# Softmax sums of the first attention with tokens on partitions, 16 reciprocals for each token, widened by GpSimd and turned by TensorE

## The chip, the core and the metric

One core of one Trainium2 chip runs the whole program in one launch. The metric is the device time of one execution in microseconds (us), the median of several runs. The engines are named as the profile names them: PE (TensorE), PEld (its weight loads), DVE (VectorE), ACT (ScalarE), POOL (GpSimd) and SP (SyncE). Each works through its own instructions in the order in which they are written and waits at semaphores for the others.

## The reference

The program is four layers of attention and feed-forward on x of 16 x 64 tokens with 128 features. Only the first attention is touched. Of it this is computed, with 16 heads of 8 features and 64 keys for each batch:

```
qh = (layernorm(x) @ Wq.T + bq)   kh = (ctx @ Wk.T + bk)   vh = (ctx @ Wv.T + bv)
scores = einsum('bhqd,bhkd->bhqk', qh, kh) / sqrt(8)
attn = softmax(scores, axis=-1)
out = einsum('bhqk,bhkd->bhqd', attn, vh)      (heads side by side: 128 features)
x = x + out @ Wo.T + bo
```

The rest of the model follows: a mixture of experts, a channel attention, a quantized matmul, a deformable attention, experts again, a masked attention and a quantized gated network. All in float32.

## The kernel before

The 1024 tokens are 8 tiles of 128. A tile is called here by its number j, and its work is spread over five consecutive rounds t of a software pipeline, `attention()` from L409, which each engine goes through in its own loop:

- Scores of tile t+1: PE multiplies queries and keys (L487), 8 matmuls, in round t.
- In round t DVE takes each head's maximum (L610) and subtracts it (L613). ACT takes the exponential of the whole tile (L552).
- In round j+1 PE turns the probabilities, so that keys lie on partitions (L501, 8 transposes), and ACT copies them from PSUM in two halves (L563) into one of two buffers `pT`.
- In round j+2 PE weighs the values (L514, 16 small matmuls, result `ps[:, 6, 0:128]`, features on partitions, tokens along the row) and makes the softmax sums (L518, 8 matmuls with a 32-column stationary operand of ones and `pT` as the moving operand of 128 columns). The sums come out in the layout of the result: each head's sum is repeated on the head's 8 partitions, for 128 tokens.
- In round j+3 DVE takes the reciprocal of 128 x 128 sums (L635) and multiplies it into the result (L637, `o_fm`). PE multiplies with Wo (L543, into `ps[:, 7]`).
- In round j+4 DVE adds the result to x (L643), and in j+5 it takes the statistics for the next layer norm (L252).

The order is the order of the code. Within a round DVE goes: scores of t, reciprocal and product of t-3, addition of t-4, statistics of t-5. PE goes: scores of t+1, transposes of t-1, values and sums of t-2, and last the projection of t-3. PE begins the values of tile j only when DVE has read tile j-1 out of that PSUM bank (semaphore `of_ready`). The hooks `experts_pe`, `experts_act` and `experts_dve` put the start of the following layer into the last rounds: the layer norm of the first 512 tokens (its second square root and DVE's factors in rounds 7 and 8, ACT's two tiles L349 in round 8), its turn on PE (L367) at the end of round 8, and the first experts' matmuls (L852, L857) at the end of round 9. The projection of tile 7 is behind those on PE. The expert layer after it is emitted in one piece and starts with a second block of L852/L857.

The branch `masked` of this function is not used in this program: the last attention has code of its own.

Of the kernel before, what the change touches and what calls it, by code (L numbers as in the profile page):

```python
# [20 lines left out]
P = 128  # L21
B, S, D = 16, 64, 128
T = B * S
NT = T // P
H, HD = 16, 8
# [90 lines left out]
def build(nc, A, out):  # L116

    ctx = ExitStack()
    with ctx:
# [130 lines left out]
        def tile_stats(j):  # L250

            return V.bn_stats(stats[:, j, :], x_tm[:, j, :])  # L252
# [156 lines left out]
        def attention(n, layer, wq, wo, bo, prepared, masked, bm_ready=None, beside_pe=nothing, beside_act=nothing,  # L409
# [18 lines left out]
            of_ready, y_ready, y_added = s("o_fm"), s("y"), s("y_added")  # L428

# [25 lines left out]
            else:  # L455
                @block.gpsimd
                def _(pool):

                    l0_norm.wait(pool)
                    pool.wait_ge(rows0_in, 16)  # L460
                    pool.wait_ge(v_sb, 4)
                    G.tensor_tensor(x_tm[:], x_tm[:], over(row(bo), 1, NT), ALU.add).then_inc(pool_chain, 1)
                    chained["pool"] += 1

# [3 lines left out]
            def _(pe):  # L468
# [36 lines left out]
                def weigh_values(j):  # L505
                    pe.wait_ge(pt_ready, 2 * j + 2)
                    if j == 0:
                        pe.wait_ge(vx_ready, 4)
                    else:
                        pe.wait_ge(of_ready, j)  # L510
# [6 lines left out]
                    for c in range(8):  # L517
                        ins = PE.matmul(ps[32 * (c // 2):32 * (c // 2) + 32, 6, 128:256], ones[:, c % 2, :],  # L518
                                        pT[j % 2][:, 128 * c:128 * c + 128], start=(c % 2 == 0), stop=(c % 2 == 1))
                    ins.then_inc(o_ready, 1)  # L520

# [4 lines left out]
                for t in range(NT + 3):  # L526
# [11 lines left out]
                    if 0 <= t - 3 < NT:  # L538
                        j = t - 3
                        pe.wait_ge(of_ready, j + 1)  # L540
                        if j >= 1:
                            pe.wait_ge(y_added, j)
                        PE.matmul(ps[:, 7, 0:128], o_fm[:, j * P:j * P + P], mat(wo), start=True, stop=True)\  # L543
                            .then_inc(y_ready, 1)
# [3 lines left out]
            def _(act):  # L548
                for t in range(NT + 2):
# [7 lines left out]
                    if 0 <= t - 1 < NT:  # L557
# [3 lines left out]
                        for k in range(2):  # L561
                            act.wait_ge(ptT_ready, 2 * j + k + 1)
                            AC.activation(pT[j % 2][:, 512 * k:512 * k + 512], ps[:, 4 + k, :], ACT.Copy)\  # L563
                                .then_inc(pt_ready, 1)
                    beside_act(act, t)
# [15 lines left out]
            def _(dve):  # L581
# [3 lines left out]
                for t in range(NT + 5):  # L585
                    if t < NT:
# [40 lines left out]
                    if 0 <= t - 3 < NT:  # L627
                        j = t - 3
                        dve.wait_ge(o_ready, j + 1)
                        if masked:  # L630

                            dve_link(V.tensor_scalar(rb, ps[:, 6, 128:256], 1.0, None, ALU.max))
                            V.reciprocal(rb, rb).then_inc(rb_ready, 1)
                        else:
                            V.reciprocal(rb, ps[:, 6, 128:256]).then_inc(rb_ready, 1)  # L635
                        dve.wait_ge(rb_ready, j + 1)
                        V.tensor_tensor(o_fm[:, j * P:j * P + P], ps[:, 6, 0:128], rb, ALU.mult).then_inc(of_ready, 1)  # L637
                    if 0 <= t - 4 < NT:
                        j = t - 4
                        if j == 0 and not masked:  # L640
                            dve.wait_ge(pool_chain, 2)
                        dve.wait_ge(y_ready, j + 1)
                        V.tensor_tensor(x_tm[:, j], x_tm[:, j], ps[:, 7, 0:128], ALU.add).then_inc(y_added, 1)  # L643
                    if 0 <= t - 5 < NT and t - 5 != 3:
                        dve.wait_ge(y_added, t - 4)
                        ins = tile_stats(t - 5)
                    if t - 4 == 3:
                        dve.wait_ge(y_added, 4)
                        dve_link(tile_stats(3))
# [2243 lines left out]
```

## Time and profile before

| | us |
|---|---|
| median of 3 runs (lowest, highest) | 464.21 (463.15, 467.38) |
| the profiled execution's own time | 463.37 |
| its span in the profile | 461.6 |
| PE busy | 398.0 (86%) |
| DVE busy | 359.8 (78%) |
| ACT busy | 253.0 (55%) |
| POOL busy | 114.5 (25%) |

The span is the profiled execution from its first to its last instruction; 1.8 us lie around it. The first attention's rounds take the stretch from about 14 to 56 us. Busy shares are those of the whole program; what the change is worth is read from that stretch alone. Matmuls overlap, so how long a group of them takes is read from the start of its first to the start of the group behind it, when nothing waits in between.

### The profile page before, as it was taken

How to read it: one execution, taken by the hardware profiler on the slowest of the kernel's cores; microseconds unless marked ns; L12 is line 12 of the kernel's file. 1: busy time of each engine (PE TensorE's matmuls, PEld its weight loads, DVE VectorE, ACT ScalarE, POOL GpSimd, SP SyncE). 2: the span in 40 equal slices, each digit the busy share in tenths (PEclk: the TensorE clock that was granted, in tenths of full speed). 3: DMA queues.
4: the chain of work that ended last, by engine and by line, in shares of the span. 5: the costliest groups of instructions: out<-in, count | busy, mean ns of one | idle time of the engine just before them, and what ended most of it. 6: DMA issues, size and time to landing. Idle time of an engine off the chain costs nothing.

```text
span 461.6 us, 8687 instructions
## 1 busy us (share of the span) xinstructions
PE 398.0 (86%) x3415; PEld 262.4 (57%) x3415; DVE 359.8 (78%) x802; ACT 253.0 (55%) x438; POOL 114.5 (25%) x97
## 2 busy tenths in 40 slices
PE   8988989999999988786787888899999999868156
PEld 5555566566666667553454546385556766643045
DVE  4799646558544587979879898999899689988985
ACT  4785753333223334456797784766766433444942
POOL 3200000006990001005995544031221023100200
PEclk9999999999999999989999999999999999989759
DMA  7890000000000000017000003000000000000001
GB/s 227 357 322 6 1 1 1 1 0 1 0 1 0 1 3 2 0 58 309 2 1 0 3 1 70 0 2 0 2 0 3 1 1 3 1 0 0 1 1 45
DMA packets 11084, 16.51 MB, mean 36 GB/s; under 512 B 5274, under 2 KB 9764, under 8 KB 10148
## 3 DMA queue, kind: packets, MB, share of 16 engines
q1 hardware_dynamic: 10756, 15.17, 9.4%
q10 hardware_dynamic: 288, 0.79, 0.6%
q8 instruction: 27, 0.44, 0.4%
q14 instruction: 13, 0.11, 0.1%
HBM read 15.43 MB, written 0.52 MB: 35 GB/s over the span
## 4 chain that ended last, share of the span: by engine, by line
PE 48%; DVE 32%; ACT 11%; issue 7%; DMA 1%; POOL 0%; ACTq 0%; DVEq 0%
PE ps L852 7%; PE ps L857 7%; PE ps L891 7%; PE ps L2119 4%; PE ps L2109 2%; PE ps L242 2%; DVE arena L1906 2%; DVE stats L252 2%; PE ps L1758 2%; PE ps L2146 1%; DVE arena L610 1%; DVE arena L613 1%; PE ps L2662 1%; DMA ctx_fm<-in_ctx_fm 1%; PE ps L2643 1%
## 5 line engine op out<-in xcount | busy, mean ns | idle before, releaser
L970 DVE SCALAR_TENSOR_TENSOR arena<-ps,cols,arena 128x512 f32<-128x512 f32 x40 | 29.7, 750 | 42.3 <-PE ps L857 38.0
L866 ACT ACTIVATE arena<-ps,cols 128x512 f32<-128x512 f32 x40 | 27.4, 687 | 63.9 <-PE ps L852 63.8
L242 PE MATMUL ps<-const 128*128 128x256 f32 x162 | 43.0, 412 | 7.4 <-ACT arena L2709 4.4
L891 PEld LDWEIGHTS ps<-weights,arena 128*128 128x128 f32 x320 | 38.6, 192 | 8.1 <-issue 8.0
L1906 DVE TENSOR_SCALAR arena<-ps 128x512 f32<-128x512 f32 x56 | 36.4, 683 | 7.3 <-PE ps L1744 3.5
L242 PEld LDWEIGHTS ps<-const 128*128 128x128 f32 x162 | 31.4, 203 | 16.3 <-ACT arena L2709 4.7
L891 PE MATMUL ps<-weights,arena 128*128 128x128 f32 x320 | 39.2, 276 | 0.2 <-DVE x_tm L959 0.2
L857 PE MATMUL ps<-h_fm,weights 128*128 128x512 f32 x80 | 37.7, 593 | 0.7 <-DVE arena L970 0.7
L852 PE MATMUL ps<-h_fm,weights 128*128 128x512 f32 x80 | 37.7, 594 | 0.6 <-ACT h_fm L373 0.6
L2109 PE MATMUL ps<-h_fm,weights 128*128 128x512 f32 x64 | 30.3, 606 | 2.7 <-ACT arena L2493 1.8
L1744 PE MATMUL ps<-l2buf,picks_b 128*128 128x256 bf16 x160 | 25.5, 275 | 6.5 <-DVE arena L1906 4.7
L2119 PEld LDWEIGHTS ps<-weights,arena 128*128 128x128 f32 x256 | 29.4, 192 | 2.6 <-issue 2.6
L2119 PE MATMUL ps<-weights,arena 128*128 128x128 f32 x256 | 30.0, 275 | 0.9 <-DVE x_tm L2336 0.9
L857 PEld LDWEIGHTS ps<-h_fm,weights 128*128 128x128 f32 x80 | 15.1, 190 | 20.2 <-issue 18.2
L1758 PE MATMUL ps<-arena,kexp 128*32 128x320 f32 x256 | 20.5, 438 | 5.3 <-ACT l2buf L1849 3.9
L1065 POOL TENSOR_TENSOR wn<-wn,winv 128x1152 f32<-128x1152 f32 x1 | 2.1, 2129 | 85.7 <-DVE winv L1055 85.7
L2493 ACT ACTIVATE arena<-ps 128x512 f32<-128x512 f32 x32 | 18.0, 597 | 9.2 <-PE ps L2109 9.1
L959 DVE SCALAR_TENSOR_TENSOR x_tm<-ps,arena,x_tm 128x128 f32<-128x128 f32 x80 | 22.4, 342 | 0.3 <-DVE stats L252 0.2
L1744 PEld LDWEIGHTS ps<-l2buf,picks_b 128*128 128x128 bf16 x160 | 12.6, 99 | 17.0 <-DVE arena L1906 10.0
L2109 PEld LDWEIGHTS ps<-h_fm,weights 128*128 128x128 f32 x64 | 11.2, 189 | 17.7 <-issue 10.2
L852 PEld LDWEIGHTS ps<-h_fm,weights 128*128 128x128 f32 x80 | 13.7, 191 | 10.4 <-issue 9.6
L2275 POOL TENSOR_TENSOR arena<-arena 128x1024 f32<-128x1024 f32 x5 | 11.5, 2301 | 31.6 <-DVE arena L2374 31.6
(401 smaller groups left out, 890.8 us busy)
## 6 DMA issues: line engine op xcount, KB each, us to landing
weights<-in_moe_w SPq DMA_DIRECT2D x2, 2048.0 KB, 10.0
weights<-in_moe_w SPq DMA_DIRECT2D x3, 1280.0 KB
l2buf<-in_picks SPq DMA_DIRECT2D x1, 1664.0 KB, 7.9
rows<-in_rows SPq DMA_DIRECT2D x1, 1024.0 KB, 13.7
x_tm<-in_x SPq DMA_DIRECT2D x2, 256.0 KB, 5.2
ctx_fm<-in_ctx_fm ACTq DMA_DIRECT2D x1, 512.0 KB, 5.9
ctx_tm<-in_ctx SPq DMA_DIRECT2D x1, 512.0 KB, 14.5
mats<-in_mats SPq DMA_DIRECT2D x1, 512.0 KB, 14.8
```

The lines of the kernel that those rows point to most:

```text
L242: PE.matmul(ps[:, bank, 0:256], ident, const[:, 0:256], start=True, stop=True)
L852: PE.matmul(ps[:, k, :], w1[:, e, P * k:P * k + P], h_fm[:, t], start=True, stop=True)\
L857: PE.matmul(ps[:, 2 + k, :], w2[:, e, P * k:P * k + P], h_fm[:, t], start=True, stop=True)\
L866: AC.activation(silu[:, k, :], ps[:, k, :], ACT.Silu, bias=bias_col(0, e, k)).then_inc(silu_ok, 1)
L891: ins = PE.matmul(ps[:, 4 + u % 2, P * t:P * t + P], glu[:, u % 2, k, P * t:P * t + P], w3[:, e, k, :], start=(k == 0), stop=(k == 1))
L959: ins = V.scalar_tensor_tensor(out=x_tm[:, j], in0=ps[:, 4 + u % 2, P * t:P * t + P], scalar=gates[:, j, e:e + 1], in1=x_tm[:, j], op0=ALU ...
L970: V.scalar_tensor_tensor(out=glu[:, u % 2, k, :], in0=ps[:, 2 + k, :], scalar=bias_col(1, e, k), in1=silu[:, k, :], op0=ALU.add, op1=ALU.m ...
L1744: ins = PE.matmul(ps[:, m % 3, 256 * i:256 * i + 256], picks_b[:, 2 * c + i, :], ixm[:, hg, 256 * half:256 * half + 256], start=True, stop ...
L1758: ins = PE.matmul(ps[32 * hl:32 * hl + 32, 4 + par, 0:NK * S], kvc[:, j, 4 * hg + hl, :], hats[:, u % 2, NK * hl:NK * hl + NK, S * (2 * i ...
L1906: V.tensor_scalar(hat_rows(u, c), ps[:, m % 3, :], 0.0, 1.0, ALU.max, ALU.min).then_inc(near_ok, 1)
L2109: PE.matmul(ps[:, n % 3, :], m2w1[:, e, P * k:P * k + P], h_fm[:, 0:T2], start=True, stop=True)\
L2119: ins = PE.matmul(at_ps, hid[:, e % 2, k, P * j:P * j + P], m2w2[:, e, k, :], start=(k == 0), stop=(k == 3))
```

## The change

- The sums change sides. 8 matmuls now have a 128 x 128 piece of `pT` as the stationary operand and two columns of ones as the moving one (`head_ones`, two heads in each piece). They write 16 columns, `ps[:, 6, 128:144]`: one sum for each token and head, with tokens on partitions.
- ACT copies the unnormalized result to `o_fm` and the 16 sums to `shares[j % 2]` as soon as PE has made them, in round j+2, behind its copies of `pT`. A new semaphore `kept` tells PE that the bank is free, and DVE that the sums are there.
- DVE takes the reciprocal of 128 x 16 at the head of round j+3.
- POOL widens the 16 reciprocals to 128 columns (`rb`), 8 instructions in all.
- PE turns `rb` with a matmul against the identity (`spread_shares`) into `ps[:, 7, 0:128]`, between the sums of tile j+1 and the projection of tile j. The projection's result goes to the same place of PSUM.
- DVE multiplies it into `o_fm` as its last step on scores in round j+3.
- DVE's addition to x and its statistics move ahead of its work on the scores of the same round.

```diff
--- before.py
+++ after.py
@@ -426,6 +426,10 @@
             ptT_ready, pt_ready = s("probsT"), s("probsT_sb")
             o_ready, rb_ready = s("o_ps"), s("sums")
             of_ready, y_ready, y_added = s("o_fm"), s("y"), s("y_added")
+            kept, rep_ps = s("kept"), s("shares_ps")
+            shares = [arena[:, 6176 + H * i:6176 + H * i + H] for i in range(2)]
+            head_ones = ones[:, 0, 0:2 * HD:HD]
+            widened = []
 
 
             if masked:
@@ -461,6 +465,14 @@
                     pool.wait_ge(v_sb, 4)
                     G.tensor_tensor(x_tm[:], x_tm[:], over(row(bo), 1, NT), ALU.add).then_inc(pool_chain, 1)
                     chained["pool"] += 1
+                    for j in range(NT):
+                        pool.wait_ge(rb_ready, j + 1)
+                        if j >= 1:
+                            pool.wait_ge(rep_ps, j)
+                        G.tensor_copy(rb.rearrange("p (h d) -> p h d", h=H), over(shares[j % 2], 2, HD))\
+                            .then_inc(pool_chain, 1)
+                        chained["pool"] += 1
+                        widened.append(chained["pool"])
 
 
 
@@ -507,7 +519,7 @@
                     if j == 0:
                         pe.wait_ge(vx_ready, 4)
                     else:
-                        pe.wait_ge(of_ready, j)
+                        pe.wait_ge(kept, j)
                     for b in range(2):
                         for c in range(8):
                             g = c // 2
@@ -515,9 +527,15 @@
                                       pT[j % 2][:, 128 * c + 64 * b:128 * c + 64 * b + 64],
                                       start=(c % 2 == 0), stop=(c % 2 == 1))
                     for c in range(8):
-                        ins = PE.matmul(ps[32 * (c // 2):32 * (c // 2) + 32, 6, 128:256], ones[:, c % 2, :],
-                                        pT[j % 2][:, 128 * c:128 * c + 128], start=(c % 2 == 0), stop=(c % 2 == 1))
+                        ins = PE.matmul(ps[:, 6, 128 + 2 * c:130 + 2 * c], pT[j % 2][:, 128 * c:128 * c + 128], head_ones,
+                                        start=True, stop=True)
                     ins.then_inc(o_ready, 1)
+
+                def spread_shares(j):
+                    pe.wait_ge(pool_chain, widened[j])
+                    if j >= 1:
+                        pe.wait_ge(y_added, j)
+                    PE.matmul(ps[:, 7, 0:128], rb, ident, start=True, stop=True).then_inc(rep_ps, 1)
 
                 scores(0)
                 l0_norm.wait_turned(pe)
@@ -537,9 +555,8 @@
                         transposes(t - 1)
                     if 0 <= t - 3 < NT:
                         j = t - 3
+                        spread_shares(j)
                         pe.wait_ge(of_ready, j + 1)
-                        if j >= 1:
-                            pe.wait_ge(y_added, j)
                         PE.matmul(ps[:, 7, 0:128], o_fm[:, j * P:j * P + P], mat(wo), start=True, stop=True)\
                             .then_inc(y_ready, 1)
                     beside_pe(pe, t)
@@ -562,6 +579,13 @@
                             act.wait_ge(ptT_ready, 2 * j + k + 1)
                             AC.activation(pT[j % 2][:, 512 * k:512 * k + 512], ps[:, 4 + k, :], ACT.Copy)\
                                 .then_inc(pt_ready, 1)
+                    if 0 <= t - 2 < NT:
+                        j = t - 2
+                        act.wait_ge(o_ready, j + 1)
+                        AC.activation(o_fm[:, j * P:j * P + P], ps[:, 6, 0:128], ACT.Copy)
+                        if j >= 2:
+                            act.wait_ge(pool_chain, widened[j - 2])
+                        AC.activation(shares[j % 2], ps[:, 6, 128:128 + H], ACT.Copy).then_inc(kept, 1)
                     beside_act(act, t)
 
             if masked:
@@ -583,6 +607,22 @@
                     guard_queries(dve, 0)
                     dve.wait_ge(bm_ready, NT)
                 for t in range(NT + 5):
+                    if 0 <= t - 3 < NT:
+                        j = t - 3
+                        dve.wait_ge(kept, j + 1)
+                        V.reciprocal(shares[j % 2], shares[j % 2]).then_inc(rb_ready, 1)
+                    if 0 <= t - 4 < NT:
+                        j = t - 4
+                        if j == 0 and not masked:
+                            dve.wait_ge(pool_chain, 2)
+                        dve.wait_ge(y_ready, j + 1)
+                        V.tensor_tensor(x_tm[:, j], x_tm[:, j], ps[:, 7, 0:128], ALU.add).then_inc(y_added, 1)
+                    if 0 <= t - 5 < NT and t - 5 != 3:
+                        dve.wait_ge(y_added, t - 4)
+                        ins = tile_stats(t - 5)
+                    if t - 4 == 3:
+                        dve.wait_ge(y_added, 4)
+                        dve_link(tile_stats(3))
                     if t < NT:
                         pr = prob[t % 3].rearrange("p (g h k) -> p g h k", g=4, h=4)
                         pr3 = prob[t % 3].rearrange("p (h k) -> p h k", h=H)
@@ -626,27 +666,9 @@
                         V.tensor_scalar(prob[j % 3], prob[j % 3], 0.0, None, ALU.max).then_inc(clean, 1)
                     if 0 <= t - 3 < NT:
                         j = t - 3
-                        dve.wait_ge(o_ready, j + 1)
-                        if masked:
-
-                            dve_link(V.tensor_scalar(rb, ps[:, 6, 128:256], 1.0, None, ALU.max))
-                            V.reciprocal(rb, rb).then_inc(rb_ready, 1)
-                        else:
-                            V.reciprocal(rb, ps[:, 6, 128:256]).then_inc(rb_ready, 1)
-                        dve.wait_ge(rb_ready, j + 1)
-                        V.tensor_tensor(o_fm[:, j * P:j * P + P], ps[:, 6, 0:128], rb, ALU.mult).then_inc(of_ready, 1)
-                    if 0 <= t - 4 < NT:
-                        j = t - 4
-                        if j == 0 and not masked:
-                            dve.wait_ge(pool_chain, 2)
-                        dve.wait_ge(y_ready, j + 1)
-                        V.tensor_tensor(x_tm[:, j], x_tm[:, j], ps[:, 7, 0:128], ALU.add).then_inc(y_added, 1)
-                    if 0 <= t - 5 < NT and t - 5 != 3:
-                        dve.wait_ge(y_added, t - 4)
-                        ins = tile_stats(t - 5)
-                    if t - 4 == 3:
-                        dve.wait_ge(y_added, 4)
-                        dve_link(tile_stats(3))
+                        o = o_fm[:, j * P:j * P + P]
+                        dve.wait_ge(rep_ps, j + 1)
+                        V.tensor_tensor(o, ps[:, 7, 0:128], o, ALU.mult).then_inc(of_ready, 1)
                     if t - 5 == 7:
                         dve_link(ins)
                     beside_dve(dve, t)
```

What stands on DVE in round 5, before and after the change (line numbers of each kernel; L610/L650 and L613/L653 are maxima and subtraction). Before:

```order
L610 TENSOR_REDUCE arena<-ps 128x2x4 x2
L613 TENSOR_TENSOR arena<-ps,arena 128x2x256 x2
L635 RECIPROCAL arena<-ps 128x128
L637 TENSOR_TENSOR o_fm<-ps,arena 128x128
L643 TENSOR_TENSOR x_tm<-x_tm,ps 128x128
L252 BN_STATS stats<-x_tm 128x6
```

After:

```order
L613 RECIPROCAL arena<-arena 128x16
L619 TENSOR_TENSOR x_tm<-x_tm,ps 128x128
L252 BN_STATS stats<-x_tm 128x6
L650 TENSOR_REDUCE arena<-ps 128x2x4 x2
L653 TENSOR_TENSOR arena<-ps,arena 128x2x256 x2
L671 TENSOR_TENSOR o_fm<-ps,o_fm 128x128
```

The reciprocal, the addition and the statistics stand now ahead of the maxima, and the product alone is left behind the subtraction.

PE in one round with scores, before, from the scores to the projection:

```order
L487 MATMUL ps<-kexp,q_fm 64x256 x8
L501 MATMUL ps<-const,arena 128x128 x8
L514 MATMUL ps<-arena,v 32x64 x16
L518 MATMUL ps<-arena,const 32x128 x8
L543 MATMUL ps<-mats,o_fm 128x128
```

After:

```order
L499 MATMUL ps<-kexp,q_fm 64x256 x8
L513 MATMUL ps<-const,arena 128x128 x8
L526 MATMUL ps<-arena,v 32x64 x16
L530 MATMUL ps<-const,arena 128x2 x8
L538 MATMUL ps<-const,arena 128x128
L560 MATMUL ps<-mats,o_fm 128x128
```

L530 (the sums) has 2 moving columns on 128 x 128 instead of 128 moving columns on 32 stationary ones, and L538 is new, between the sums and the projection L560.

ACT from round 4 on; before it has the exponential (L552) and the two copies of `pT` (L563) in each round:

```order
L552 ACTIVATE arena<-arena 128x1024
L563 ACTIVATE arena<-ps 128x512 x2
L552 ACTIVATE arena<-arena 128x1024
L563 ACTIVATE arena<-ps 128x512 x2
L552 ACTIVATE arena<-arena 128x1024
```

After:

```order
L569 ACTIVATE arena<-arena 128x1024
L580 ACTIVATE arena<-ps 128x512 x2
L585 ACTIVATE o_fm<-ps 128x128
L588 ACTIVATE arena<-ps 128x16
L569 ACTIVATE arena<-arena 128x1024
```

The two copies that end in `kept` come behind the exponential and the copies of `pT` of the same round.

## Rows read from the trace of the kernel before

**Rows 1.** The page's first line, for the whole program.
```profile
span 461.6 us, 8687 instructions
```

**Rows 2.** Chain that ended last, 35 to 46 us, by line.
```profile
by line: DVE arena L613 27.5%; DVE arena L635 26.4%; DVE arena L610 21.6%; issue 7.5%; PE ps L514 5.4%; DVE x_tm L643 5.0%; DVE o_fm L637 4.0%; DVE stats L252 3.7%; DVEq L616 0.6%
```

**Rows 3.** Timeline, DVE: start us, length us, engine, line, op, tiles, shapes, count, idle before.
```profile
24.80 1.29 DVE L610 TENSOR_REDUCE arena<-ps 128x8 f32<-128x512 f32 x2 [0.24 <-DVE arena L613]
...
37.17 1.27 DVE L610 TENSOR_REDUCE arena<-ps 128x8 f32<-128x512 f32 x2
...
39.77 0.96 DVE L635 RECIPROCAL arena<-ps 128x128 f32<-128x128 f32 x1
...
41.37 1.27 DVE L610 TENSOR_REDUCE arena<-ps 128x8 f32<-128x512 f32 x2
...
44.98 0.29 DVE L637 TENSOR_TENSOR o_fm<-ps,arena 128x128 f32<-128x128 f32 x1
...
55.90 0.29 DVE L643 TENSOR_TENSOR x_tm<-x_tm,ps 128x128 f32<-128x128 f32 x1 [2.39 <-PE ps L543]
```

**Rows 4.** Timeline, PE matmuls, 20 to 58 us, same columns.
```profile
26.35 0.64 PE L518 MATMUL ps<-arena,const 128*32 128x128 f32 x15
27.47 1.41 PE L487 MATMUL ps<-kexp,q_fm 32*64 32x256 f32 x16 [0.47 <-issue]
...
30.91 0.49 PE L543 MATMUL ps<-mats,o_fm 128*128 128x128 f32 x2
...
35.19 1.42 PE L487 MATMUL ps<-kexp,q_fm 32*64 32x256 f32 x16
36.55 1.09 PE L501 MATMUL ps<-const,arena 128*128 128x128 f32 x8
37.57 0.68 PE L514 MATMUL ps<-arena,v 128*32 128x64 f32 x31
...
38.07 0.64 PE L518 MATMUL ps<-arena,const 128*32 128x128 f32 x15
38.64 0.49 PE L543 MATMUL ps<-mats,o_fm 128*128 128x128 f32 x2
39.06 1.42 PE L487 MATMUL ps<-kexp,q_fm 32*64 32x256 f32 x16
...
42.51 0.49 PE L543 MATMUL ps<-mats,o_fm 128*128 128x128 f32 x2
...
45.41 0.65 PE L514 MATMUL ps<-arena,v 128*32 128x64 f32 x30 [1.54 <-DVE o_fm L637]
...
49.43 0.63 PE L367 MATMUL ps<-const,h_tm 128*128 128x128 f32 x4
...
52.05 1.88 PE L852 MATMUL ps<-h_fm,weights 128*128 128x512 f32 x4
...
55.48 0.38 PE L543 MATMUL ps<-mats,o_fm 128*128 128x128 f32 x2
```

**Rows 5.** Timeline, ACT, 15 to 58 us, same columns.
```profile
27.27 1.07 ACT L563 ACTIVATE arena<-ps 128x512 f32<-128x512 f32 x2
...
39.72 1.06 ACT L552 ACTIVATE arena<-arena 128x1024 f32<-128x1024 f32 x1 [1.33 <-DVEq L616]
...
48.48 0.87 ACT L349 ACTIVATE h_tm<-x_tm,shift,rstd 128x128 f32<-128x128 f32 x2
```

**Rows 6.** Timeline, PE matmuls, 60 to 72 us: the gate's logits.
```profile
66.77 1.85 PE L904 MATMUL ps<-gate_w,h_fm 128*128 128x8 f32 x16
68.47 2.03 PE L891 MATMUL ps<-weights,arena 128*128 128x128 f32 x16
```

**Rows 7.** Groups by line and shape, DVE: busy us, mean ns of one, idle before.
```profile
L1235 DVE RECIPROCAL arena<-arena 128x16 f32<-128x16 f32 x2 | 0.5, 253 | 0.1
```

**Rows 8.** Groups by line and shape, ACT, same columns.
```profile
L1427 ACT ACTIVATE wT<-ps 128x128 f32<-128x128 f32 x1 | 0.3, 271 | 0.0
```

**Rows 9.** Groups by line and shape, POOL, same columns.
```profile
L1108 POOL CAST bkv_parts<-rows 96x256 bf16<-96x256 f32 x1 | 0.4, 399 | 0.1
```

## The prediction

> **What bounds the kernel now.** I read four views of the stretch from 14 to 56 us, in this order. The chain of waits comes first: from 35 to 46 us it runs through DVE's maxima (L610), subtraction (L613) and reciprocal (L635), with hardly any PE in it [rows 2]. So in the steady rounds DVE sets the pace. DVE's timeline says by how much: the maxima of tile 6 start at 37.17 and those of tile 7 at 41.37, a round of 4.20 us, 0.96 of it the reciprocal of 128 x 128 [rows 3]. PE's timeline shows a second resource close behind. Its round from 35.19 to 39.06 is 3.87 us, and its parts follow each other with no gap between them: scores 1.36, transposes 1.02, values 0.50, sums 0.57, projection 0.42 [rows 4]. PE had run ahead of DVE and pays it back once, 1.54 us at 45.41, where it waits for `o_fm` [rows 4]. ACT is last: exponential and copies are a little over 2 us of each round, and before the exponential it waits 1.33 us for DVE [rows 5].
>
> What the reader should take from this: DVE has only 0.33 us on PE. A change that frees DVE by a full reciprocal and gives PE more than that much work moves the bound to PE.
>
> **The change part by part.** Durations are start to start, or from the start of one to the start of what it releases.
>
> DVE, removed: the reciprocal, 0.96 us, and its small gap. Added: a reciprocal of 128 x 16, 0.25 us from the same shape at L1235 [rows 7]. The product keeps its size; its operands are now PSUM and `o_fm`. Net about 0.7 us less for each tile, if DVE still were the bound.
>
> PE, sums: 8 matmuls of one 128 x 128 float32 stationary each. The trace has the nearly identical form in the logits: 8 matmuls, 16 records, 128 x 128 stationary, 8 moving columns. They take from 66.77 to 68.47, 1.70 us, or 0.106 us for each record [rows 6]. Each float32 matmul is two records here, so the sums become 1.70 instead of 0.57 us, 1.13 more for each tile. Bounds: at the pace of the values, 32 records in 0.50 us [rows 4], 16 records would be 0.25 us. If the loads of two columns could not hide behind matmuls as those of eight do, twice the row is my ceiling, 3.4 us. I take 1.70, since this row has the same stationary and the same work of loading, and differs only in 8 columns against 2.
> The Trainium skill (TensorE: Matmul & The Clock Gate, Back-to-back issue gap) gives a warm isolated gap of about 60 cycles (25 ns) for 1 to 64 moving columns. By it alone 16 records would be 0.4 us, and the sums would become cheaper than before. The logits' 0.106 us for each record speak against it: with a fresh 128-column stationary each time, something other than the columns sets the pace.
>
> PE, turning the shares: one more 128 x 128 float32 matmul, the form of the projection, 0.42 us [rows 4]. But it stands in a chain inside the round: from its start to DVE's product 0.42 us, as from the last projection at 55.48 [rows 4] to the addition at 55.90 [rows 3]; and from the product to PE's next matmul 0.43 us, as 44.98 [rows 3] to 45.41 [rows 4]. In that second 0.43 PE stands still, since the projection right behind it needs the product, and behind that are the next scores. The round on PE becomes 1.36 + 1.02 + 0.50 + 1.70 + 0.42 + 0.43 + 0.42 = **5.85 us** instead of 3.87, and without scores 4.49.
>
> ACT: two copies more, 128 x 128 at 0.27 us [rows 8] and 128 x 16 somewhere between 0 and 0.27; I take 0.2. ACT has room for 0.47 us. Their place costs more than their length, because DVE now begins its round by waiting for them. This closes a loop: reciprocal 0.25, addition and statistics 0.4 (from the reciprocal at 39.77 to the next maxima at 41.37 lie 1.60 us, 0.96 of them the reciprocal and the rest three short instructions, 0.2 each [rows 3]), then 2.55 from the maxima at 37.17 [rows 3] to the exponential at 39.72 [rows 5], exponential 1.0, copies of `pT` 1.07 [rows 5], the two new copies 0.47: about **5.7 us**. Even with free sums DVE could not go back to 4.20 while scores are left.
>
> POOL: 8 copies of 128 x 128, POOL's row for 96 x 256 is 0.40 us [rows 9], so 0.2 to 0.4 us. DVE's reciprocal comes at the head of a round and PE turns the shares 4.6 us later, so this is free up to some 3 to 4 us. Without that cover each microsecond would lie in PE's round.
>
> **The sum**, as a walk through PE. The sums of tile 0 start at 26.35 and now end at 28.05 instead of about 27, so the scores of tile 4 start at 28.05 instead of 27.47 [rows 4]. On the other side DVE may not begin the maxima of tile 3 at 24.80 [rows 3] any more. It waits for the sums of tile 0, which ACT keeps behind the copies from 27.27 to 28.34 [rows 5], that is at 28.8; with the reciprocal it starts at 29.1, 4.3 us later. Subtraction ends 2.5 us later at 31.6, before PE's turned shares of tile 0 (28.05 + 1.36 + 1.02 + 0.50 + 1.70 + 0.42 = 33.05). PE is the later one.
> - Projection of tile 0: 28.05 + 5.85 - 0.42 = 33.48; before 30.91 [rows 4], 2.6 later.
> - Projection of tile 3: three rounds on, 51.03; before 42.51, **8.5 later**. Three rounds at 1.98 more are 5.9 of it.
> - Round 7, no scores: projection of tile 4 at 55.52. DVE subtracts tile 7 until 54.6; the exponential, the copies of tile 6 and the kept sums follow until 57.2, and the transposes of tile 7 must wait for those copies, so that they end at 57.4. Values 0.50, sums 1.70, turn and product 0.85: projection of tile 5 at 60.45.
> - Layer norm for the first half: DVE computes its factors after that product (0.3), ACT applies them in 0.87 [rows 5], so PE's turn stands at 61.75; before 49.43, 12.3 later.
> - Values, sums, turned shares, product and projection of tile 6, then the experts' first matmuls at 65.7; before 52.05, 13.6 later.
> - Tile 7 behind them: the old distance 55.48 - 52.05 = 3.43, plus 0.85 for turn and product: 69.95; before 55.48, **14.5 later**.
>
> All that follows (addition, statistics, second layer norm, the experts, which are bound by PE) waits for this point and has the same work as before, so I carry the whole 14.5 us to the end. The profiled execution's own time is 463.37 (span 461.6 [rows 1], 1.8 around it), so this one gives 477.9; the median of the runs is 0.84 higher and would give 478.7. I forecast 478.5 us.
>
> **The rivals.**
> - *The sums are cheap, and the loop through ACT and DVE holds.* If 16 records cost 0.25 us, PE's round is 4.4, and the 5.7 us loop sets rounds 4 to 6 while PE sets those behind. For it: the values run at 0.016 us for each record. Against it: rows 6. Rounds with scores lose only 0.15 each, rounds without scores about 1.3 less: some 2.5 to 3 us below my sum, 475.5. Chance 0.10. This is also what the gap of the Trainium skill (TensorE: Matmul & The Clock Gate, Back-to-back issue gap) would make of the sums, with 0.4 us for them.
> - *Weight loads do not overlap.* The sums at 3.4 us, 1.7 us more on each of 8 tiles: 13.6 us more, 492. For it: only that two columns leave less time to hide a load than eight. Chance 0.04.
> - *DVE's relief wins: faster.* PE has 0.33 us of slack and DVE 0.7 us to give for each tile. If the sums ran at 0.25 us, and if the shares of a tile were kept before DVE asks for them, DVE's round would fall to about 3.5 in four rounds, and the last four reciprocals would leave PE's path with 0.7 each: 5.7 us less, 458. The point from which it decides is the loop of 5.7 us falling below 4.20, that is ACT keeping the sums ahead of the exponential of the round, which the code does not do. Chance 0.03.
> - *The delay is absorbed.* The end of the attention is late, but a transfer or POOL work bounds later stages, so that most comes back. For it: the projection of tile 7 already waited 3.43 us behind other matmuls. Against it: those matmuls are late by nearly as much, as their operands come from this same attention. 464. Chance 0.02.
> - *POOL's copy with repeated reads is slow*, over 4 us for each tile. Each further microsecond is 8 at the end. Chance 0.02, 485 and more.
>
> What remains, 0.79, is my forecast.
>
> **The numbers.** Within the forecast the waits between engines that the old trace shows only once are good for 0.3 us on each of 8 tiles, 2.5 us up or down, and the three runs shown lie up to 4 us apart. The range from 475 to 483 holds the forecast and the cheap sums, and leaves out the two expensive and the two fast cases. A measurement of this kernel can tell about 1% from no change. Faster by over 1%: 0.03. Within 1%: 0.02. Slower by over 1%: 0.95.
>
> **What would show it right or wrong.** In the changed profile: the sums as 16 records of about 0.106 us each from their first start to that of the matmul behind them; PE's rounds with scores near 5.9 us and a gap of 0.4 us before each projection, ended by DVE's product; DVE's maxima of tile 3 near 29 us instead of 24.80, with a wait for ACT's small copy ahead of them; the projection of tile 7 near 70 us. The prediction is wrong if the sums take under 1 us, if PE's longest idle times are ended by POOL, or if the stages behind 70 us are shorter than they were.

## The result

The changed kernel takes 505.59 us (median of 4 runs, 503.88 to 507.35) against 464.22 before. The ratio is 1.0846, with a 95% interval of 1.0792 to 1.09. The forecast was 478.5 with a range of 475 to 483: the side was right, the size was not. The change costs 41.4 us, almost three times the 14.3 us forecast (478.5 - 464.21).

### The profile page after: what moved, and what is told of

Read it like the earlier page. It is cut to its first block, busy times and chain, and to the rows that moved or that the text cites. A ratio compares the mean times of both kernels' runs of the same rounds, so it can differ in the third digit from the quotient of the medians.

```text
span 502.1 us, 8751 instructions
## 1 busy us (share of the span) xinstructions
PE 437.3 (87%) x3431; PEld 296.0 (59%) x3431; DVE 353.7 (70%) x802; ACT 255.6 (51%) x454; POOL 116.8 (23%) x105
## 4 chain that ended last, share of the span: by engine, by line
PE 54%; DVE 27%; ACT 10%; issue 6%; DMA 1%; POOL 0%; ACTq 0%; DVEq 0%
PE ps L874 7%; PE ps L913 7%; PE ps L879 7%; PE ps L530 5%; PE ps L2141 4%; PE ps L513 2%; PE ps L2131 2%; PE ps L242 2%; PE ps L499 2%; DVE arena L1928 2%; PE ps L1780 2%; PE ps L526 2%; DVE stats L252 2%; PE ps L2168 1%; DMA ctx_fm<-in_ctx_fm 1%
## 5 line engine op out<-in xcount | busy, mean ns | idle before, releaser
L913 PEld LDWEIGHTS ps<-weights,arena 128*128 128x128 f32 x320 | 40.1, 198 | 8.1 <-issue 8.0
L913 PE MATMUL ps<-weights,arena 128*128 128x128 f32 x320 | 40.9, 283 | 0.2 <-DVE x_tm L981 0.2
L874 PE MATMUL ps<-h_fm,weights 128*128 128x512 f32 x80 | 39.0, 610 | 0.6 <-ACT h_fm L373 0.6
L879 PE MATMUL ps<-h_fm,weights 128*128 128x512 f32 x80 | 37.7, 593 | 0.7 <-DVE arena L992 0.7
L2131 PE MATMUL ps<-h_fm,weights 128*128 128x512 f32 x64 | 30.3, 606 | 2.7 <-ACT arena L2515 1.9
L671 DVE TENSOR_TENSOR o_fm<-ps,o_fm 128x128 f32<-128x128 f32 x8 | 2.3, 292 | 41.6 <-PE ps L538 41.6
L2141 PEld LDWEIGHTS ps<-weights,arena 128*128 128x128 f32 x256 | 29.4, 192 | 2.6 <-issue 2.6
L2141 PE MATMUL ps<-weights,arena 128*128 128x128 f32 x256 | 30.0, 275 | 0.9 <-DVE x_tm L2358 0.9
L879 PEld LDWEIGHTS ps<-h_fm,weights 128*128 128x128 f32 x80 | 15.1, 190 | 20.4 <-issue 18.4
L530 PEld LDWEIGHTS ps<-const,arena 128*128 128x128 f32 x128 | 23.3, 281 | 1.2 <-issue 1.0
L530 PE MATMUL ps<-const,arena 128*128 128x2 f32 x128 | 24.0, 318 | 0.0
L1766 PEld LDWEIGHTS ps<-l2buf,picks_b 128*128 128x128 bf16 x160 | 12.6, 99 | 17.0 <-DVE arena L1928 10.0
L2131 PEld LDWEIGHTS ps<-h_fm,weights 128*128 128x128 f32 x64 | 11.2, 189 | 17.7 <-issue 10.2
```

Source lines behind the costliest of these rows:

```text
L530: ins = PE.matmul(ps[:, 6, 128 + 2 * c:130 + 2 * c], pT[j % 2][:, 128 * c:128 * c + 128], head_ones, start=True, stop=True)
L874: PE.matmul(ps[:, k, :], w1[:, e, P * k:P * k + P], h_fm[:, t], start=True, stop=True)\
L879: PE.matmul(ps[:, 2 + k, :], w2[:, e, P * k:P * k + P], h_fm[:, t], start=True, stop=True)\
L913: ins = PE.matmul(ps[:, 4 + u % 2, P * t:P * t + P], glu[:, u % 2, k, P * t:P * t + P], w3[:, e, k, :], start=(k == 0), stop=(k == 1))
L1766: ins = PE.matmul(ps[:, m % 3, 256 * i:256 * i + 256], picks_b[:, 2 * c + i, :], ixm[:, hg, 256 * half:256 * half + 256], start=True, stop ...
L2131: PE.matmul(ps[:, n % 3, :], m2w1[:, e, P * k:P * k + P], h_fm[:, 0:T2], start=True, stop=True)\
```

## The profile after

First the page of the changed kernel: its span, the busy time of each engine, and TensorE's granted clock in 40 equal slices of 12.6 us, in tenths.

```profile
span 502.1 us, 8751 instructions
...
PE 437.3 (87%) x3431; PEld 296.0 (59%) x3431; DVE 353.7 (70%) x802; ACT 255.6 (51%) x454; POOL 116.8 (23%) x105
...
PEclk9985556899899999999899999999999999999859
```

The same clock row of the kernel before:

```profile
PEclk9999999999999999989999999999999999989759
```

The span grew by 40.5 us, from 461.6 [rows 1] to 502.1. The new thing is in the clock row. Before, the slices of the first attention all read 9; now the third to seventh read 8 5 5 5 6. PE's busy time grew by 39 us. That would look like work, yet PE has only 16 instructions more. Stretches of 10 us say where (columns: stretch, length, busy us and count for PE, PEld, DVE, ACT, POOL, then granted clock, DMA share, GB/s):

```profile
20.00:30.00 10.00, 8.58 (x115) 5.74 (x108) 5.50 (x11) 7.94 (x18) 2.13 (x2) 0.98 1.05 362
30.00:40.00 10.00, 9.56 (x103) 7.21 (x105) 4.39 (x10) 3.65 (x7) 0.30 (x1) 0.67 0.36 119
40.00:50.00 10.00, 9.56 (x68) 7.00 (x59) 3.32 (x8) 2.19 (x6) 0.30 (x1) 0.50 0.00 0
...
70.00:80.00 10.00, 9.49 (x78) 8.58 (x77) 1.51 (x10) 5.51 (x12) 0.30 (x1) 0.63 0.01 2
80.00:90.00 10.00, 8.65 (x60) 7.05 (x61) 2.41 (x12) 3.00 (x6) 0.59 (x2) 0.54 0.00 0
...
130.00:140.00 10.00, 10.00 (x51) 7.96 (x52) 4.23 (x10) 1.38 (x2) 0.00 (x0) 0.83 0.00 0
```

Between 40 and 70 us PE is busy for over 9.5 us of each 10, and the granted clock is 0.50, the lower of TensorE's two levels (1.2 instead of 2.4 GHz). It is at 0.54 between 80 and 90 us once more. It also dips to 0.83 at 130 to 140, in the middle of the expert layer. In stretches of 1 us it first falls between 29 and 30 us, behind the first sums and the scores after them, is back at 0.98 to 1.00 from 33 to 36, and falls again between 36 and 37.

PE's timeline of the changed kernel, with the first sums and one whole round (start us, length us, engine, line, op, tiles, shapes, count, idle before and what ended it):

```profile
26.30 1.95 PE L530 MATMUL ps<-const,arena 128*128 128x2 f32 x16
28.18 1.42 PE L499 MATMUL ps<-kexp,q_fm 32*64 32x256 f32 x16
...
45.85 2.36 PE L499 MATMUL ps<-kexp,q_fm 32*64 32x256 f32 x16
48.14 1.97 PE L513 MATMUL ps<-const,arena 128*128 128x128 f32 x8
50.04 1.10 PE L526 MATMUL ps<-arena,v 128*32 128x64 f32 x32
51.07 3.58 PE L530 MATMUL ps<-const,arena 128*128 128x2 f32 x16
54.51 0.77 PE L538 MATMUL ps<-const,arena 128*128 128x128 f32 x2
55.66 0.80 PE L560 MATMUL ps<-mats,o_fm 128*128 128x128 f32 x2 [0.38 <-DVE o_fm L671]
56.39 2.36 PE L499 MATMUL ps<-kexp,q_fm 32*64 32x256 f32 x16
```

And its end:

```profile
88.71 3.05 PE L874 MATMUL ps<-h_fm,weights 128*128 128x512 f32 x4
...
94.08 0.49 PE L560 MATMUL ps<-mats,o_fm 128*128 128x128 f32 x2 [0.38 <-DVE o_fm L671]
```

These rows stand beside [rows 4]. The round from 45.85 to 56.39 is 10.54 us instead of 3.87. *Every* part has grown, also those the change did not touch: scores 2.29 us instead of 1.36, transposes 1.90 instead of 1.02, values 1.03 instead of 0.50. The sums take 3.44 us. The first sums, at 26.30, took 1.88 until the scores at 28.18, while the clock was still 1.00. The projection of tile 7 starts at 94.08, 38.6 us later than in [rows 4], and the experts' first matmuls at 88.71 instead of 52.05.

DVE and ACT at the head of the first changed round, and DVE's product:

```profile
28.67 0.25 DVE L613 RECIPROCAL arena<-arena 128x16 f32<-128x16 f32 x1 [4.28 <-ACT arena L588]
28.84 1.23 DVE L650 TENSOR_REDUCE arena<-ps 128x8 f32<-128x512 f32 x2
...
55.32 0.29 DVE L671 TENSOR_TENSOR o_fm<-ps,o_fm 128x128 f32<-128x128 f32 x1 [6.49 <-PE ps L538]
```

```profile
28.29 0.28 ACT L585 ACTIVATE o_fm<-ps 128x128 f32<-128x128 f32 x1
28.46 0.18 ACT L588 ACTIVATE arena<-ps 128x16 f32<-128x16 f32 x1
```

```profile
35.53 0.30 POOL L472 COPY arena<-arena 128x128 f32<-128x128 f32 x1 [6.25 <-DVE arena L613]
```

As forecast, the maxima of tile 3 start at 28.84 instead of 24.80 [rows 3], behind ACT's copies (0.28 and 0.18 us). The reciprocal of 16 columns takes 0.25, POOL's copy 0.30. In the steady round DVE idles 6.49 us until PE has turned the shares. DVE is relieved, and it buys nothing.

## The experiments

Three theories were on trial. Theory A: the sums load a 128 x 128 stationary operand for every 2 moving columns, and after such a stretch TensorE is granted its lower clock. Theory B: the pause in which PE waits for the product brings the clock down. Theory C: the clock explains nothing, the added work is simply longer than priced.

**Wide sums (e1).** The changed kernel, with 128 moving columns instead of 2. The operand is a row of zeros with the two columns of ones at place 2c, and the 8 matmuls accumulate. The pause of PE stays. Lines that let POOL write this operand once, and the waits for it, are left out here.

```diff
-                        ins = PE.matmul(ps[:, 6, 128 + 2 * c:130 + 2 * c], pT[j % 2][:, 128 * c:128 * c + 128], head_ones,
-                                        start=True, stop=True)
+                        ins = PE.matmul(ps[:, 6, 128:256], pT[j % 2][:, 128 * c:128 * c + 128],
+                                        near_ones[:, 126 - 2 * c:254 - 2 * c], start=(c == 0), stop=(c == 7))
```

> The changed kernel with one thing altered: each matmul of the sums moves 128 columns (126 of them zero, accumulated over the 8 matmuls) instead of 2. Stationary operands, their number, the order, the turn by PE and its wait for the product are as in the changed kernel. Theory A (the sums move too few columns, and TensorE's clock falls to its lower level for that): the granted clock stays 1.00 in the rounds, the 16 records of the sums take about 1.9 us, a round with scores about 6.0 us, the projection of tile 7 stands near 71 us, and the time is 478 to 481 us. Theory B (the 0.4 us in which PE waits for the product in each round make the clock fall): those waits are still there, so the clock stays near 0.5 and the time near 505 us. Theory C (the clock is not the matter, the sums and the turn are simply longer than I took them to be): as B, 505 us or a little more.

Measured: 483.58 us (4 runs) beside 467.28 for the kernel before, ratio 1.0367, interval 1.0298 to 1.0437. So 64 times the moving columns take some 22 us *off* the changed kernel (1.0846 to 1.0367 of the kernel before). Two stretches of it, and one round and the end on PE's timeline:

```profile
25.00:28.00 3.00, 3.00 (x41) 2.50 (x41) 0.00 (x0) 3.00 (x6) 0.00 (x0) 0.50 1.12 341
42.19:48.26 6.07, 5.63 (x78) 4.22 (x77) 3.32 (x8) 2.36 (x5) 0.29 (x2) 1.00 0.00 0
```

```profile
42.19 1.42 PE L502 MATMUL ps<-kexp,q_fm 32*64 32x256 f32 x16
...
45.18 2.05 PE L535 MATMUL ps<-near_ones,arena 128*128 128x128 f32 x16
47.07 0.39 PE L543 MATMUL ps<-const,arena 128*128 128x128 f32 x2
47.84 0.49 PE L565 MATMUL ps<-mats,o_fm 128*128 128x128 f32 x2 [0.38 <-DVE o_fm L676]
48.26 1.42 PE L502 MATMUL ps<-kexp,q_fm 32*64 32x256 f32 x16
...
73.44 0.49 PE L565 MATMUL ps<-mats,o_fm 128*128 128x128 f32 x2 [0.38 <-DVE o_fm L676]
```

The round from 42.19 to 48.26 is 6.07 us at a clock of 1.00, the sums in it 1.89, the pause of 0.38 before the projection still there. Theories B and C would have left the time at 505. The time is 2.6 us above the range I gave for A. In the profiled execution (485.15 us) the clock was at 0.50 between 25 and 28 us, before the first wide sums had run, and the transposes took 1.86 instead of about 1.0 us there. It came back in the first wide sums and then held. So this first fall is no work of the sums. PE had just waited 1.26 us; the kernel before has the same wait and stayed at 1.00 in its profile, and what decides between the two is not shown.

**Filling the pause (e2, e3).** One or three matmuls of 256 columns in PE's wait for the product. The edit of e2 is shown, e3 has `range(3)`:

```diff
                         spread_shares(j)
+                        if t < NT + 2:
+                            pe.wait_ge(sc_read, 2 * min(t, NT - 1) + 2)
+                            for _ in range(1):
+                                PE.matmul(ps[:, 2 * (t % 2) * (t < NT), 0:256], ident, const[:, 0:256], start=True, stop=True)
                         pe.wait_ge(of_ready, j + 1)
```

> The changed kernel with one matmul of 256 moving columns, whose result nobody reads, in PE's wait for the product (0.43 us at the higher clock, so it costs about nothing). Theory A (too few moving columns): columns are added, but fewer than the change took away, so the clock may come back only in part: between 480 and 505 us. Theory B (the wait itself): the wait is filled, the clock stays 1.00 and the time is 478 to 480 us.

> As the run before with three such matmuls in each round instead of one: 2 x 0.43 us more of work in 7 rounds, 6 us at the higher clock. Theory A: 768 moving columns more, enough for the clock to stay at its higher level in most rounds, so 484 to 488 us in spite of the added work. Theory C: added work on PE's path only makes it longer, 515 us and more.

Measured, one run each: 506.62 us with one, 490.21 with three. One stretch of the run with one:

```profile
45.00:50.00 5.00, 5.00 (x25) 3.97 (x25) 1.20 (x5) 0.35 (x2) 0.29 (x1) 0.50 0.00 0
```

The pause is gone, PE is busy for all 5 us, the clock is 0.50, and nothing is won. That speaks against B for this kernel. With three, PE does more work and the program is 15 us shorter than the changed kernel. Two stretches of the run with three:

```profile
33.00:38.00 5.00, 5.00 (x21) 4.73 (x22) 0.45 (x2) 0.91 (x4) 0.30 (x1) 0.50 0.10 25
46.58:53.30 6.72, 6.67 (x83) 5.29 (x82) 3.32 (x8) 2.27 (x5) 0.29 (x1) 1.00 0.01 2
```

Early on the clock fell to 0.50 too, then it came back, and a whole round from 46.58 to 53.30 with all its additional work is 6.72 us. The transposes of the early stretch begin at 29.71 and its projection ends at 39.64, 9.93 us; the same parts take 5.36 us from 47.94 to 53.30. By this estimate the stretch cost 4.6 us, and without it the time would lie in the range of 484 to 488.

**The sums alone, on the kernel before (e5, e6).** DVE, ACT, POOL and the order are those of the kernel before; 8 matmuls with the stationary operands of the changed kernel are added in each round, once with 2 and once with 128 moving columns. The edit of e5 is shown:

```diff
+                    for c in range(8):
+                        PE.matmul(ps[:, 6, 256:258], pT[j % 2][:, 128 * c:128 * c + 128], const[:, 0:2],
+                                  start=True, stop=True)
                     for c in range(8):
                         ins = PE.matmul(ps[32 * (c // 2):32 * (c // 2) + 32, 6, 128:256], ones[:, c % 2, :],
```

> The kernel before, with 8 matmuls more in each round ahead of its own sums: stationary 128 x 128 pieces of the turned probabilities as in the changed kernel, 2 moving columns, result read by nobody. Nothing else of the change: DVE, ACT and POOL do what they did. Theory A (few moving columns bring the clock down): the clock falls below 1.00 in the rounds though PE never waits long, a round with scores is 8 to 10 us, and the time is 485 to 500 us. Theory B (only waits of PE do it): PE is busier than before, so the clock stays 1.00, a round is 3.87 + 1.75 = 5.6 us and the time 474 to 478 us.

> As the run before, but with 128 moving columns in each of the 8 added matmuls: 1.9 us of work a round instead of 1.75. Theory A: the clock stays 1.00, a round with scores is 3.87 + 1.9 = 5.8 us, and the time is 475 to 480 us, that is less than with 2 columns although more is computed. Theory C (it is only the length of the work): the same as with 2 columns or slightly more.

Measured, one run each beside 465.1 for the kernel before: **503.1 us with 2 columns, 480.93 with 128**. Two stretches with 2 columns, the second of them a whole round, then added sums in two rounds, the kernel's own sums behind them, and the projection of tile 7:

```profile
40.00:45.00 5.00, 5.00 (x53) 3.75 (x53) 2.71 (x6) 2.25 (x3) 0.00 (x0) 0.50 0.02 3
...
49.25:59.73 10.48, 10.42 (x91) 7.72 (x91) 4.13 (x9) 2.25 (x3) 0.00 (x0) 0.50 0.01 2
```

```profile
36.11 1.95 PE L518 MATMUL ps<-const,arena 128*128 128x2 f32 x16
...
54.47 3.58 PE L518 MATMUL ps<-const,arena 128*128 128x2 f32 x16
57.98 1.10 PE L521 MATMUL ps<-arena,const 128*32 128x128 f32 x16
...
92.71 0.38 PE L546 MATMUL ps<-mats,o_fm 128*128 128x128 f32 x2
```

The same with 128 columns:

```profile
41.01:47.00 5.99, 5.94 (x91) 4.40 (x91) 4.13 (x9) 2.15 (x3) 0.00 (x0) 1.00 0.02 4
```

```profile
44.01 2.05 PE L518 MATMUL ps<-const,arena 128*128 128x128 f32 x16
45.99 0.67 PE L521 MATMUL ps<-arena,const 128*32 128x128 f32 x16
...
70.72 0.38 PE L546 MATMUL ps<-mats,o_fm 128*128 128x128 f32 x2
```

With 2 columns PE is busy for 10.42 of 10.48 us, has no wait at all, and the granted clock is 0.50. With 128 columns it is busy for 5.94 of 5.99 and the clock is 1.00. The 16 records, with the same stationary operands, take 3.51 us in the one and 1.98 in the other. 38 of the 41 us of the whole change appear when only these 8 matmuls are added in each round, and 22 of them go away when the columns become 128. The kernel before varied by 3 us over its 7 runs (464.02 to 466.98), so one run of each is enough for a difference of 22. This shows theory A without the rest of the change. Theory C is right about the 16 us that stay with 128 columns, and wrong about the 22.

One more thing stands in the profile with 2 columns. As in e1, the first fall came before the first added sums: the values at 25.52 already took 1.01 us to 26.53, against 0.62 with 128 columns. But then the clock came back, and the sums at 36.11 took 1.88 us. By 40 us it was at 0.50 again, and the timeline shows no wait of PE in between. With 128 columns the first fall did not come in e6; in e1 it came, and then the clock returned and stayed. So the narrow sums are not needed for the first fall; they go with the fall that comes again and lasts, and B has no pause for that one.

The Trainium skill (TensorE: Matmul & The Clock Gate, Part 1: The HAM clock gate) says that the gate follows how busy PE has been recently. If busy is read as the profile's busy time, this case does not agree: 10.42 of 10.48 us were busy at a clock of 0.50. In that round 3.51 us of the busy time are 16 records of 2 moving columns each.

**The order alone (e4).** The changed order of DVE and ACT, with the old sums. POOL's widening and PE's turn are left out, and the reciprocal is one of 128 x 128 again, now at the head of the round:

```diff
-                        ins = PE.matmul(ps[:, 6, 128 + 2 * c:130 + 2 * c], pT[j % 2][:, 128 * c:128 * c + 128], head_ones,
-                                        start=True, stop=True)
+                        ins = PE.matmul(ps[32 * (c // 2):32 * (c // 2) + 32, 6, 128:256], ones[:, c % 2, :],
+                                        pT[j % 2][:, 128 * c:128 * c + 128], start=(c % 2 == 0), stop=(c % 2 == 1))
...
-                        dve.wait_ge(rep_ps, j + 1)
-                        V.tensor_tensor(o, ps[:, 7, 0:128], o, ALU.mult).then_inc(of_ready, 1)
+                        dve.wait_ge(rb_ready, j + 1)
+                        V.tensor_tensor(o, shares[j % 2], o, ALU.mult).then_inc(of_ready, 1)
```

> The order of the changed kernel alone: the sums stay as they were before the change (32-column stationary ones, 128 moving columns), ACT copies result and sums, DVE takes the reciprocal of 128 x 128 at the head of the next round, then adds and takes statistics, and multiplies behind the subtraction; no work on POOL, no turn by PE. The loop through DVE and ACT that I priced at 5.7 us has 0.96 for the reciprocal here instead of 0.25 and 0.1 more for the copy: 6.5 us a round instead of 4.20, so the projection of tile 7 at about 67 to 70 us and a time of 475 to 479 us. Theory A: the clock stays 1.00, since all matmuls move 64 columns or more. Theory B: PE waits over 2 us in each round, so the clock falls and the time is above 485 us.

Measured: 477.38 us (one run) beside 467.28 for the kernel before, and the projection of tile 7 at 69.55. DVE's reciprocals in two rounds, three of PE's projections, and two stretches:

```profile
40.39 0.95 DVE L605 RECIPROCAL arena<-arena 128x128 f32<-128x128 f32 x1 [2.05 <-ACT arena L580]
...
46.56 0.95 DVE L605 RECIPROCAL arena<-arena 128x128 f32<-128x128 f32 x1 [2.05 <-ACT arena L580]
```

```profile
32.85 0.49 PE L552 MATMUL ps<-mats,o_fm 128*128 128x128 f32 x2 [1.92 <-DVE o_fm L663]
...
50.73 0.69 PE L552 MATMUL ps<-mats,o_fm 128*128 128x128 f32 x2 [2.23 <-DVE o_fm L663]
...
69.55 0.38 PE L552 MATMUL ps<-mats,o_fm 128*128 128x128 f32 x2
```

```profile
39.60:44.98 5.38, 4.35 (x75) 2.58 (x74) 3.97 (x8) 1.58 (x4) 0.00 (x0) 0.90 0.00 0
50.73:57.21 6.48, 4.51 (x58) 3.47 (x58) 4.31 (x11) 2.35 (x6) 0.00 (x0) 0.51 0.00 0
```

The loop through DVE and ACT is real: 6.17 us from reciprocal to reciprocal, where I had 6.5, and DVE waits 2.05 us for ACT's copy in each. The projection of tile 7 is 14.07 us later than before, about as much as I had forecast for the whole change. That is not the price of the place of the kept sums by itself, since this loop also holds the reciprocal of 0.95 us, where the changed kernel has 0.25. One part of A's expectation missed: the clock did not stay at 1.00. It was 0.51 from 50.73 to 57.21, a stretch in which PE was busy for only 4.51 of 6.48 us. In this run the clock was lower behind PE's waits of 1.92 and 2.23 us, with no narrow matmul in the rounds. That fits B for pauses of this length, but no run takes them away alone. The 0.38 us of the changed kernel are another matter: e1 keeps them and the clock stays at 1.00.

**Projection later (e7).** Wide sums, and the projection behind the next scores, so that PE does not wait for the product.

```diff
                     if t + 1 < NT:
                         scores(t + 1)
+                    if 0 <= t - 4 < NT - 1 and t + 1 < NT:
+                        project(t - 4)
...
                         spread_shares(j)
-                        pe.wait_ge(of_ready, j + 1)
-                        PE.matmul(ps[:, 7, 0:128], o_fm[:, j * P:j * P + P], mat(wo), start=True, stop=True)\
-                            .then_inc(y_ready, 1)
```

> The kernel with 128 moving columns in its sums, and PE's projection of a tile moved behind the next scores (behind the next transposes where there are no scores left), so that DVE's product has time and PE does not wait for it. My term for that wait was 0.43 us in each of 8 rounds; the trace with wide sums shows 0.38. If it is on the path: rounds with scores of 5.7 instead of 6.07 us, and about 2.5 to 3 us less than with wide sums alone, 478 to 481 us. If DVE's later addition delays the next round by as much: no change.

Measured: 487.94 us beside 465.1 for the kernel before, ratio 1.0482, interval 1.0445 to 1.052. The gain did not come. The interval lies just above that of wide sums alone (1.0298 to 1.0437), so it is rather a loss. PE's scores in two rounds, the transposes of tile 7, the last projection:

```profile
39.51 1.42 PE L502 MATMUL ps<-kexp,q_fm 32*64 32x256 f32 x16
...
44.98 1.42 PE L502 MATMUL ps<-kexp,q_fm 32*64 32x256 f32 x16
...
57.82 1.62 PE L516 MATMUL ps<-const,arena 128*128 128x128 f32 x8 [2.19 <-ACT arena L593]
...
74.74 0.49 PE L541 MATMUL ps<-mats,o_fm 128*128 128x128 f32 x2 [0.38 <-DVE o_fm L684]
```

The rounds became shorter, 5.47 us from 39.51 to 44.98 against 6.07. The gain was given back where the scores run out: PE waits 2.19 us for ACT's copies before the transposes at 57.82. DVE's addition now waits for the later projection, and with it come maxima, exponential and copies: the maxima of tile 7 start 8.58 us after PE began its scores (53.56 less 44.98), against 6.90 in e1. Behind that wait the clock was lower for once, and the parts up to 63.06 took some 1.5 us more than the same parts elsewhere in this run. At the end the projection of tile 6 had moved behind the experts' matmuls, and the turn of tile 7 waited 0.47 us for DVE's addition. The last projection is at 74.74, 1.3 us behind the 73.44 of e1. The pause was on PE's path, and the loop of DVE and ACT was right behind it.

**Reciprocals on POOL (e8).** A version meant to beat both: order and matmuls of the kernel before, ACT copies the sums of tiles 0 to 4, POOL raises them to the power -1.

```diff
+                    for j in range(5):
+                        pool.wait_ge(copied, j + 1)
+                        G.tensor_tensor(rbs[j % 2], rbs[j % 2], one128, ALU.pow).then_inc(rb_ready, 1)
```

> A version meant to be faster than both: the order and the matmuls of the kernel before, but for tiles 0 to 4 ACT copies the 128 x 128 sums to SBUF (0.27 us) and POOL, idle here, raises them to the power -1; DVE only multiplies. Tiles 5 to 7 stay as they were. DVE's rounds fall from 4.20 to about 3.2 us, PE with 3.87 becomes the bound. If POOL needs less than about 3 us for a tile: 1.5 to 2 us faster than before, 462 us on the same footing as 464. If it needs over 4 us: slower by the excess in each of five rounds.

Measured: 569.49 us (6 runs, five of them from 565.24 to 570.40 and one at 685.72), ratio 1.2246.

```profile
28.73 20.80 POOL L469 TENSOR_TENSOR arena<-arena 128x128 f32<-128x128 f32 x1 [6.50 <-ACT arena L576]
```

One power of 128 x 128 takes 20.80 us on POOL. So the last case of the expectation came about, for each of five tiles. No version here beats the kernel before.

## Why the prediction was wrong

**The step that failed** is the price of every matmul in the rounds. Each was read at a granted clock of 1.00, the sum of 5.85 us for a round took that for given, and none of the rivals was the clock. The logits' row gave the time of one such group nearly right (1.70 against 1.88 us at a clock of 1.00), but those 8 matmuls stood alone between wide ones. Here the same form comes in every round. From about 30 us on, but for two stretches of 3 to 4 us, the rounds ran at the lower clock, and the steady one took 10.54 us.

The projection of tile 7, forecast 14.5 us later, came 38.6 later. The pieces:

- 14.5 us as priced at a clock of 1.00. e1, with the clock at 1.00, has a round of 6.07 us beside the 5.85 forecast.
- 1.9 us of mis-sized terms. In e1 the projection is at 73.44; without the 1.6 us that its transposes, values and sums lost at half clock near 25 to 28 us it would be at 71.9 instead of 69.95. Most of it is the sums: 1.89 us for 16 records where the logits' row gave 1.70, in each of 8 tiles. The values take 0.62 instead of 0.50, and turn and product 0.77 instead of 0.85.
- 22.2 us of the lower clock, taken as the rest: 94.08 less 71.9. The pair e5 and e6 gives the same size by itself, 22 us.

Behind that point another 1.9 us were added (span 40.5 against 38.6). The clock's dip to 0.83 at 130 to 140 us stands there, where the kernel before, 40 us earlier, has 1.00. No experiment took that dip away, so its share is not shown.

Point by point:

- *DVE is relieved, PE becomes the bound*: right. The pause before each projection is 0.38 where I had 0.43, and it is ended by DVE's product.
- *Maxima of tile 3 near 29 us, behind ACT's small copy*: right, 28.84.
- *POOL's copies cost nothing*: right, 0.30 us each and no wait of PE for them.
- *The loop of DVE and ACT, 5.7 us*: near in size, 6.17 in e4 with the longer reciprocal and 5.47 for a round of e7; in the changed kernel PE was slower and hid it.
- *Sums 1.70 us, round 5.85*: 1.89 and 6.07 at a clock of 1.00 (e1); 3.44 and 10.54 as it ran.
- *All of the delay reaches the end*: right, nothing was absorbed.
- Of the rivals, weight loads that do not hide (492) came nearest in size, by the wrong mechanism: at a clock of 1.00 the 2-column records took 1.88 us in the changed kernel, and the 128-column ones 1.89 in e1.

## What to carry to other kernels

Matmuls with few moving columns are not cheap for it, and they can cost far more than their own time. Here 16 records with 2 columns took as long as 16 with 128, and with them in every round the clock was low under all the other matmuls, while the profile still called PE busy. Before turning an operand round to save work on another engine, ask how many columns each load of a stationary operand serves after the change. If the form must stay, try it with a wide moving operand: 128 columns took 1.89 us where 2 took 1.88, and the program was 22 us shorter. And when a step that was late in an engine's round is moved to its head, price the whole loop that it closes, not the instruction.

## What the runs showed of the hardware

- 16 records with a 128 x 128 float32 stationary operand took 1.88 us with 2 moving columns (changed kernel, e5) and 1.89 to 1.98 with 128 (e1, e6), all at a clock of 1.00. In the changed kernel and e5, at 0.50, those with 2 columns took 3.44 to 3.51.
- PE busy for 10.42 of 10.48 us, without a wait, at a granted clock of 0.50 (e5): a full busy row does not mean the higher clock.
- PE busy for 4.51 of 6.48 us without narrow matmuls, behind a wait of 2.23 us (e4): 0.51 as well.
- The clock was at 0.50 from 25 to 28 us in e1, before its first wide sums, and at 1.00 there in the kernel before, with the same work and the same wait of 1.26 us.
- POOL's power of 128 x 128 float32: 20.80 us, against 0.30 for a copy of the same size.
